# Banded attention in runs of 32 keys and 64 queries instead of blocks of 128 keys and 160 queries

## The reference, cut to what matters

```python
def local_gqa_attn(x, wq, wk, wv, wo):
    q = split_heads(x @ wq, H)                     # H = 16 heads of 8
    k = split_heads(x @ wk, KVH)                   # KVH = 4
    v = split_heads(x @ wv, KVH)
    q, k = (rope(q, BASE_L), rope(k, BASE_L))
    q, k = (qk_norm(q), qk_norm(k))
    k, v = (repeat_kv(k), repeat_kv(v))
    i = jnp.arange(x.shape[1])
    diff = i[:, None] - i[None, :]
    mask = (diff >= 0) & (diff < WIN)              # WIN = 32
    return merge_heads(sdpa(q, k, v, mask)) @ wo
```

## Time and profile before

| | us |
|---|---|
| median of 3 runs (1787.54 to 1792.34) | 1788.07 |
| profiled execution | 1787.96 |
| its span | 1786.1 |
| the stage's first and last instruction | 1497.5, 1575.4 |

### The profile page before, as it was taken

The page is one execution under the profiler, slowest core; times in us unless marked ns, Lnnn a source line. Parts: engine busy times, 40 slices in busy tenths (PEclk is TensorE's granted clock), DMA queues, the critical chain, the costliest instruction groups (busy, mean ns, idle before and its releaser), DMA issues. The chain is left out here.

```text
span 1786.1 us, 25074 instructions
## 1 busy us (share of the span) xinstructions
PE 1624.6 (91%) x8849; PEld 887.3 (50%) x8849; DVE 981.1 (55%) x2214; ACT 817.5 (46%) x1338; POOL 354.1 (20%) x492
## 2 busy tenths in 40 slices
PE   7989977999998997999799989998799977979998
PEld 2436654344444664445444545666333344545665
DVE  7673447888872434535644453446533447963444
ACT  5643323566674332432233343222688856743221
POOL 1314232223232432201320032002300100032000
PEclk9999987999998998999899989998899988989999
DMA  4643024110104101000000016553311024105554
GB/s 110 235 119 108 20 70 139 46 55 28 55 8 184 58 21 37 1 1 1 1 0 1 1 31 142 126 112 86 93 36 34 18 52 131 48 31 129 116 112 95
DMA packets 56221, 120.22 MB, mean 67 GB/s; under 512 B 8439, under 2 KB 35095, under 8 KB 51299
## 3 DMA queue, kind: packets, MB, share of 16 engines
q1 hardware_dynamic: 53628, 113.55, 23.8%
q0 software_dynamic: 2432, 5.00, 0.8%
q10 hardware_dynamic: 39, 0.07, 0.0%
HBM read 85.38 MB, written 19.96 MB: 59 GB/s over the span
## 5 line engine op out<-in xcount | busy, mean ns | idle before, releaser
L2471 DVE TENSOR_REDUCE a_most<-psum 128x1 f32<-128x512 f32 (+3 forms) x304 | 180.1, 654 | 42.6 <-PE psum L2317 31.7
L2429 ACT ACTIVATE a_probs<-psum 128x512 f32<-128x512 f32 (+1 forms) x304 | 153.0, 584 | 86.4 <-PE psum L2347 85.7
L3304 ACT ACTIVATE t_silu<-psum 128x512 f32<-128x512 f32 x136 | 81.2, 597 | 240.5 <-PE psum L3362 239.4
L3379 PEld LDWEIGHTS psum<-t_slot,t_hid 128*128 128x128 f32 x1024 | 132.1, 191 | 55.9 <-issue 49.7
L2732 ACT ACTIVATE ga_probs<-psum 128x1024 f32<-128x1024 f32 (+2 forms) x160 | 138.5, 950 | 24.3 <-PE psum L2646 24.1
L3475 DVE TENSOR_TENSOR t_prod<-t_silu,psum 128x512 f32<-128x512 f32 x104 | 71.5, 688 | 137.4 <-ACT t_silu L3304 137.4
L3379 PE MATMUL psum<-t_slot,t_hid 128*128 128x128 f32 x1024 | 134.4, 276 | 2.9 <-DVE t_hid L3466 2.9
L3362 PE MATMUL psum<-xnT,t_slot 128*128 128x512 f32 x256 | 131.2, 594 | 3.1 <-ACT t_silu L3304 3.1
L3367 PE MATMUL psum<-xnT,t_slot 128*128 128x512 f32 x256 | 130.8, 592 | 0.0
L2314 PE MATMUL psum<-a_ks,a_qs 96*128 96x512 bf16 (+3 forms) x384 | 119.4, 342 | 4.7 <-DVE a_most L2471 2.7
L2347 PE MATMUL psum<-a_qs,a_ks 128*128 128x512 bf16 (+3 forms) x384 | 110.4, 327 | 4.8 <-ACT a_probs L2429 2.1
(11 more groups left out here) (453 smaller groups left out, 3014.8 us busy)
## 6 DMA issues: line engine op xcount, KB each, us to landing
t_spread<-factors SPq DMA_DIRECT2D x64, 512.0 KB, 6.5
m_experts<-experts_dram SPq DMA_DIRECT2D x14, 768.0 KB, 9.3
c_halves<-xnT SPq DMA_DIRECT2D x48, 128.0 KB, 2.3
t_slot<-experts_dram SPq DMA_DIRECT2D x32, 192.0 KB, 5.4
a_qs<-scratch_q SPq DMA_DIRECT2D x16, 288.0 KB
a_ks<-scratch_k SPq DMA_DIRECT2D x24, 192.0 KB
ga_qs<-scratch_q SPq DMA_DIRECT2D x16, 288.0 KB
la_qs<-scratch_q SPq DMA_DIRECT2D x16, 288.0 KB
```

The lines of the kernel that those rows point to most:

```text
L2429: act.activation(probs[:, (n * BLOCKS + b) % PROBS, h0:h0 + heads, 0:wide], src, ACT.Exp, scale=SCALE).then_inc(probs_ready, 1)
L2471: v.tensor_reduce(most[:, row, h0:h0 + heads, qt % KPH], src, AX.X, ALU.max).then_inc(max_read, 1)
L3379: ins = pe.matmul(core.psum[:, c, t * P:(t + 1) * P], left[:, t * P:(t + 1) * P], weights, start=pair < 0 and t == 0, stop=False, skip_gro ...
```

## The change

The block of keys is cut to 32 (`SUB`), and with it the queries that see it to 64 (`REACH`). Four runs of 32 keys stand on the four quarters of the partitions, so that 128 keys need 4 heads x 64 columns; two such blocks fill a bank of 512 columns and make a step (`PER_UNIT` = 2). A group has 4 steps, the stage 32 (`STEPS`), each with one bank of scores; four banks are in turn.

- Scores: for each run one product, with the run's 32 keys as weights at tile position (0, 32*j), and the four heads' 64 queries as 256 moving columns. Where the 64 queries cross query 512 or the end, there are two products of half the width.
- ScalarE and VectorE take a step's 512 columns at once. `keep` is 64 wide, made in four pieces of 32 partitions.
- Values: `vslot` has a copy for each of the four runs, in which only the run's 32 rows hold values and the other 96 are zero. Each run is multiplied for each head with 64 columns of queries. GpSimd clears four times as much and copies each group's values in four pieces.
- The copies, turnings and normalisings of the halves stand one to two steps behind the values; the turning of the first half now comes in the next group's step 0.
- The projection has banks of its own (`TURN_BANK`, `Y_BANK`). Chunks 0 and 1 are projected at steps 17 to 23 (`PROJECT`), in the loop; chunks 2 and 3 behind it.

```diff
+    SUB = 32
+    SUBS = P // SUB
+    REACH = SUB + window
+    PER_UNIT = CH // (G * REACH)
+    UNITS = KT // PER_UNIT
+    STEPS = GROUPS * UNITS
     PROBS = 4
     LAG = 2
-    SLOTS = 3
-    O_BANK = 6
-    WIDE = P + window
...
+    SLOTS = 4
+    TURN_BANK, Y_BANK, O_BANK = 4, 5, 6
+    PROJECT = {GPB * UNITS + 1: 0, GPB * UNITS + 4: 1}
...
-        vslot = core.sb(ctx, tag + "vslot", [P, 2, KT, 32])
-        probs = core.sb(ctx, tag + "probs", [P, PROBS, G, WIDE])
+        vslot = core.sb(ctx, tag + "vslot", [P, 2, SUBS, KT, 32])
+        probs = core.sb(ctx, tag + "probs", [P, PROBS, PER_UNIT, G, REACH])
...
+        def pieces(k0):
+
+            cuts = sorted({k0, min(k0 + REACH, T)} | {edge for edge in range(0, T, CH) if k0 < edge < k0 + REACH})
+            return list(zip(cuts, cuts[1:]))
...
-            s.chain(g.memset(vslot[:, :, :, :], 0.0))
-            s.chain(g.memset(vslot[:, :, :, HD:HD + 1], 1.0))
+            s.chain(g.memset(vslot[:, :, :, :, :], 0.0))
+            for j in range(SUBS):
+                s.chain(g.memset(vslot[SUB * j:SUB * (j + 1), :, j, :, HD:HD + 1], 1.0))
...
-                g.tensor_copy(vslot[:, n % 2, :, 0:HD], v_all[:, n // GPB * KT:(n // GPB + 1) * KT, a:a + HD]).then_inc(vslot_ready, 1)
+                for j in range(SUBS):
+                    rows = slice(SUB * j, SUB * (j + 1))
+                    g.tensor_copy(vslot[rows, n % 2, j, :, 0:HD], v_all[rows, n // GPB * KT:(n // GPB + 1) * KT, a:a + HD]).then_inc(vslot_ready, 1)
...
+                for i in range(PER_UNIT):
+                    for j in range(SUBS):
+                        k0 = (u * PER_UNIT + i) * P + j * SUB
...
+                        for x, (lo, hi) in enumerate(parts):
+                            ins = pe.matmul(dst[:, :, at:at + hi - lo], ks[:, n % RING, k0:k0 + SUB], qs[:, n % RING, lo // CH, :, lo % CH:lo % CH + hi - lo],
+                                            start=i == 0 and x == 0, stop=i == PER_UNIT - 1 and x == len(parts) - 1,
+                                            tile_position=(0, SUB * j), skip_group_check=True)
+                            at += hi - lo
                 ins.then_inc(score_pe, 1)
...
+                for i in range(PER_UNIT):
+                    kt = u * PER_UNIT + i
+                    for j in range(SUBS):
+                        k0 = kt * P + j * SUB
+                        for lo, hi in pieces(k0):
+                            if n and k0 < CH and lo == CH:
+                                pe.wait_ge(o_ready, 2 * n)
+                            for hh in range(G):
+                                ins = pe.matmul(core.psum[32 * hh:32 * hh + 32, O_BANK + lo // CH, lo % CH:lo % CH + hi - lo], vslot[:, n % 2, j, kt, :],
+                                                probs[:, step % PROBS, i, hh, lo - k0:hi - k0], start=lo % CH == 0 and (k0 == 0 or lo > k0),
+                                                stop=(k0 + SUB) % CH == 0 and lo == k0, tile_position=(0, 32 * hh), skip_group_check=True)
                 ins.then_inc(pv_pe, 1)
...
+            for step in range(STEPS):
+                n, u = divmod(step, UNITS)
+                scores(step)
+                if step >= LAG:
+                    values(step - LAG)
+                if u == 0 and n:
+                    turn(n - 1, 0)
+                if u == 2 and n:
+                    turn(n - 1, 1)
+                if step in PROJECT:
+                    c = PROJECT[step]
+                    pe.wait_ge(o_ready, 2 * GPB - 1 + c)
+                    project_turn(c, TURN_BANK)
+                if step - 2 in PROJECT:
...
+                    project(c, Y_BANK)
+            values(STEPS - 2)
+            turn(GROUPS - 1, 0)
+            values(STEPS - 1)
+            pe.wait_ge(o_ready, 2 * GROUPS - 1)
+            project_turn(NC - 2, TURN_BANK)
             turn(GROUPS - 1, 1)
...
+            project(NC - 1, 1)
```

More of the change, by code:

```diff
@@ L2887, in scores @@
                     pe.wait_ge(stack_in[n % RING], STACK * (n // RING + 1))
[L2888 to L2898, removed]
@@ L2905, in values @@
+                ins.then_inc(score_pe, 1)
+            def values(step):
+                n, u = divmod(step, UNITS)
+                pe.wait_ge(masked, step + 1)
+                if u == 0:
+                    pe.wait_ge(vslot_ready, SUBS * (n + 1))
                     if n == 0:
                         tail.read(pe)
-                    if n:
+                    else:
                         pe.wait_ge(o_ready, 2 * n - 1)
-                if kt == KPH - 1 and n:
-                    pe.wait_ge(o_ready, 2 * n)
@@ L2911, in values @@
[L2911 to L2917, removed]
-                                        probs[:, (n * KT + kt) % PROBS, hh, a - lo:b - lo], start=a % CH == 0 and (kt == 0 or a > lo), stop=kt in (KPH - 1, KT - 1),
-                                        tile_position=(0, 32 * hh), skip_group_check=True)
+                for i in range(PER_UNIT):
[9 more added lines that the diff above has]
+                                                stop=(k0 + SUB) % CH == 0 and lo == k0, tile_position=(0, 32 * hh), skip_group_check=True)
@@ new lines, in project @@
+            def project(c, bank):
+                pe.wait_ge(oT_ready, c + 1)
+                for t in range(TPC):
+                    ins = pe.matmul(core.psum[:, bank, t * P:(t + 1) * P], core.xnT[:, c * CH + t * P:c * CH + (t + 1) * P], w_out, start=True, stop=True)
+                ins.then_inc(y_pe, 1)
+            for step in range(STEPS):
+                n, u = divmod(step, UNITS)
+                scores(step)
[10 more added lines that the diff above has]
+                if step - 2 in PROJECT:
+                    c = PROJECT[step - 2]
+                    if c == 0:
+                        pe.wait_ge(w_out_in, 16)
+                    else:
+                        pe.wait_ge(y_added, c)
+                    project(c, Y_BANK)
@@ L2951, in _ @@
[L2951 to L2957 removed]
+            project_turn(NC - 1, 0)
+            project(NC - 1, 1)
         @block.scalar
@@ L2961, in copy_o @@
             def copy_o(n, half):
[L2962 removed]
+                act.wait_ge(pv_pe, n * UNITS + UNITS // 2 * (half + 1))
                 if n:
@@ L3002, in _ @@
             v.wait_ge(masks_in, 16)
-            a, n = MASK_COLS["band"]
-            v.tensor_scalar(keep[:, :], masks[:, a:a + n], -1.0, None, ALU.is_ge).then_inc(keep_ready, 1)
-            v.wait_ge(keep_ready, 1)
+            a, _n = MASK_COLS["band"]
+            for j in range(SUBS):
+                rows = slice(SUB * j, SUB * (j + 1))
+                v.tensor_scalar(keep[rows, :], masks[rows, a + SUB * j:a + SUB * j + REACH], -1.0, None, ALU.is_ge).then_inc(keep_ready, 1)
             tail.vector(v, 1)
```

141 lines of the change are left out of this document (61 added, 80 removed).

## The result

The changed kernel takes 1794.85 us (median of 14 runs, 1792.07 to 1797.74) against 1789.73 (1786.98 to 1793.05) for the kernel before beside it: ratio 1.0026, 95% interval 1.0018 to 1.0034. It is slower, by about a quarter of a per cent; 1774.2 had been forecast.

The account below looks back on a forecast made before the run. VectorE was taken to bound the loop, TensorE close behind. A 54.4 us loop from 1501.8 and a 5.4 us tail end the stage at 1561.6, against 1575.4: 1787.96 - 13.8 = 1774.2 us, range 1767 to 1797.

Parts of the forecast that it names:

- What bounds the kernel: Changed stage's loop before the change: VectorE bounds it at 1.0 us per block of 128 keys, TensorE close behind.
- DMAs: Loads and TensorE's code in the stage: some 20 code packets, one in 2.5 us, taken as hidden.
- forecast loop: Changed stage from first values at 1501.8: 53.0 us of terms plus 1.4 for waits, 54.4 us.
- The open price, per pair: TensorE's front end: a load-multiplication pair every 22 ns, 14 within values, taken at full column speed; break-even 27.5 ns.
- Code that arrives late at times: 1779 to 1794: Rival on TensorE's supply in the stage: late code or rates of 24 to 30 ns, 1779 to 1794 us; chance 0.13.
- front end: Rival: TensorE starves between short matmuls; at 36 ns a pair 1809 us; chance 0.15 for 30 ns and more.
- The estimate of 1797: Scores and values at 25 ns for each of 2384 multiplications: 60 us instead of 37, ending near 1797.
- scores made one behind another: Rival: the four score tiles don't run side by side, 30 us instead of 7.5, 1797 us; chance 0.04.
- Values, scores, turnings: TensorE's work in the loop: values 29.5 us, scores 7.5 us side by side, turnings 10.5 us.
- Cold clock: TensorE at the loop's start: 4.6 us at half speed after the first values, 2.3 us lost.
- Start: GpSimd's fourfold clearing and copies before the first values: ready about 1501 to 1501.5, costed at nothing.
- Tail: From the loop's end to the stage's end: 5.4 us where there were 9.2.

Follow-up runs that it names:

- e12: Changed kernel without the stack loads of groups 2 to 7, whose scores use the stacks of groups 0 and 1; 1792.52 us, 1.0011.
- e3: Changed kernel with the value multiplications of two of a group's four heads left out; 1773.39 us, 0.9916 of the kernel before.
- e2: Changed kernel with the same instructions, but each value multiplication over a quarter of its columns (16 of 64); 1800.56 us, 1.0058 of the kernel before.
- e1: Changed kernel with runs of 64 keys and 96 queries in place of 32 and 64; 1786.06 us, 0.9974 of the kernel before.
- e7: Changed kernel with 64-key, 96-query runs, 32-key score tiles, values three steps behind scores, all four projections behind the loop; 1775.22 us, 0.9909.
- e5: Changed kernel with runs of 64 keys and 96 queries, scores made in column tiles of 32 keys; 1781.55 us, 0.9946 of the kernel before.
- e10: Changed kernel with exponentials and values in bf16, halving the values' instructions, all products made; 1766.14 us, 0.9872 of the kernel before.

## Why the prediction was wrong, step by step

*What bounds the kernel* (VectorE, with TensorE close behind): right. Once VectorE's 50 us of masks were 22, TensorE decided alone.

*The step that failed* is the one under DMAs: "2500 pairs need some 20, one in 2.5 us ... Taken as hidden". The count was right (19 packets in the loop), the cover wrong. I had set the packet's place on the queues against a DMA capacity that was nearly idle, and not the time from the asking for a packet to its use against the time in which TensorE uses one up. No row of before puts a packet closer than 6.8 us to the next; the view of 1540 to 1570 has three in 30 us (slices of 0.75 us):

```profile
GB/s 0 0 0 22 0 0 0 0 0 0 0 0 0 0 0 22 0 0 0 0 0 0 0 0 0 0 0 22 0 0 0 0 0 0 0 0 0 0 0 0
```

One in 2.5 us (2.7 by the prediction's own loop of 54.4) was thus asked of it nowhere, just as with the pairs; I bounded the one and not the other. What the runs showed in place of "hidden": e12's loop took 67.9 us for its 19 packets, 3.6 each with nothing else in the queues for most of it, and this one 72.2, with up to 5.4 us between two packets while the stacks are loaded. The loss of 17.8 us against the forecast loop is 15.6 us of spells and 2.2 of the rest. Against e3's loop of 49.8, which is fed, it is 22.4: 15.6 of spells and 1.8 of the fallen clock. Most of the other 5 can be estimated. A spell is counted from the end of the multiplication before it, 0.2 us behind its start, while in a fed row the next one starts at once; fourteen times that is 3 us. And the lower clock at the start (0.58 in 1504 to 1508 in e3) covers some 3 us less of e3's values than of this loop, 1 to 1.5 us.

*The open price, per pair:* the lower bound, the full speed of the columns, was right in kind. Within a packet four tiles of 64 columns start every 56 ns and nothing between them is late. "*Code that arrives late at times: 1779 to 1794*" named the mechanism, as a rival of small size; it was neither rare nor small. The *front end* rival had the right time (it had one price a pair: 243 loads and multiplications in 3.55 us are 29 ns a pair, and 2480 pairs then 72.5 us) by the wrong mechanism: evenly spaced multiplications were not seen. The estimate of 1797 from the Trainium skill's "TensorEngine Tiling (Array Packing)" comes near, since it also counts multiplications and not columns; e2 shows that it isn't a price of each, since there 72 of a quarter of the columns start within 0.69 us, 10 ns each, where the prediction took 25 from that section, and then TensorE stops. That 1794.85 us lies inside the stated range is luck: its upper end stood there for scores made one behind another, which did not happen.

*Values, scores, turnings:* right. A step without turning takes 1.07 us where 1.2 were forecast (scores 1547.61 to 1548.68), one with turning 1.81 (1539.74 to 1541.55) where 1.9 were. Scores run side by side on four tiles, and no time is lost between them and the values.

*Cold clock:* forecast until 4.6 us after the first values; by the 0.53 of 1504 to 1508 (0.72 in the kernel before) the lower level lasted 5.9 us, 0.7 us more lost. The second fall, behind the spells, was not forecast.

*Start:* "I cost it at nothing" is the second term that failed, by 1.7 us. The prediction asked whether GpSimd would be ready in time, and it was, by 1499.7. It did not ask what the longer clearing does to VectorE, which the cover (splitting and first mask) stands on: VectorE's first piece of the mask took 1.81 us, as long as the clearing. With half the clearing (e1, 0.95 us) the first values come 4.5 us after the start, with a quarter (before) 4.3, with all of it 6.0.

*Tail:* right, 3.8 us saved.

## What to carry to other kernels

Count the instructions of TensorE, not only their columns: here the code of a straight stream came no faster than a packet of 243 loads and multiplications in about 3.5 us (3.3 at the least and 3.6 on average with empty queues), 14 to 15 ns for each, and an fp32 product is four of them. Idle time "issue" that recurs whatever the operation, together with a 16 KB packet of the instruction queue 2.2 to 2.9 us ahead of the end of each spell, is the sign of that limit. Where it holds, coarser runs are worth more than fewer columns: 64 keys with 96 queries, scores in tiles as wide as the values', and three steps of distance (e7, fp32, all products made) beat both kernels, 1775.2 us, 0.9% under the one before. And an operation that only prepares, such as the clearing on GpSimd here, can lengthen one on VectorE beside it: look at the shortest and the longest time of a line, not only at its sum.

## What the runs showed of the hardware

- Between a row of matmuls on tiles of 64 columns and one on tiles of 32, TensorE loses 0.12 us (e1, scores to values 0.28 us, e5 0.16), about what the earlier trace rows gave between 128 and 32 (0.13).
- VectorE's TENSOR_SCALAR for the mask, started 0.04 us behind a clearing on GpSimd, lasts until just after the clearing's end: 1.81 us beside 1.81 (after), 0.97 beside 0.95 (e1), 0.58 beside 0.53 (before). With no long clearing beside it, 32 partitions with 64 columns take 0.18 to 0.19 us, and 64 with 96 take 0.21.
- With the spells the clock can fall too. From 1520 to 1540 it is 1.00 in e3 (no spells), 0.91 in the changed kernel (15.6 us of them in the loop) and 0.74 in e2 (24.4); but in e12, with 13.6 us of spells and none over 1.6 us, it stays at 1.00.
- The mask's multiplication takes 0.696 us over 512 columns with probabilities in bf16 (e10) as in fp32 (0.697); the mask itself is fp32 in both.
